# Attention, GRU and experts kernel: the preparation written into the same block as the recurrence, with mean squares from the layer norm's variance and two of four batches prepared inside the first units

## The reference

```
x = x + tanh(g_xattn) * xattn(layernorm(x), ctx)
    # xattn: slots = layernorm(x); k, v = rmsnorm(ctx) @ Wk.T, @ Wv.T; three times:
    #   scores = (rmsnorm(slots) @ Wq.T) @ k.T * D**-0.5
    #   attn = softmax(scores, axis=-2)
    #   attn = attn / (sum(attn, -1) + 1e-6); updates = attn @ v
    #   slots = gru_cell(updates, slots, wih, whh, bih, bhh)
x = x + tanh(g_ffn) * ffn(layernorm(x))
    # ffn: 16 experts, each takes its 512 best tokens; plus a shared expert
```

## Time and profile before

| what | value |
| --- | --- |
| median of 3 runs | 1162.04 us (1161.96 to 1163.13) |
| the profiled execution | 1162.68 us, of which the span is 1160.9 us |
| PE busy | 1101.3 us (95%) |
| DVE, ACT, POOL busy | 69%, 48%, 31% |
| mean granted clock of PE | 0.97 |
| chain that ended last | PE 87%, DVE 6%, ACT 1%, issue 1%, POOL 1% |

### The profile page before, as it was taken

One profiled execution on the slowest core, in us unless ns is written; L12 is line 12 of the kernel. 1 busy time (PEld: TensorE's weight loads), 2 busy tenths in 40 slices (PEclk: granted clock), 3 DMA queues, 4 the chain that ended last, 5 costly groups with the idle time before them and its releaser, 6 DMA issues.

```text
span 1160.9 us, 18197 instructions
## 1 busy us (share of the span) xinstructions
PE 1101.3 (95%) x6151; PEld 951.5 (82%) x6151; DVE 798.2 (69%) x1533; ACT 555.7 (48%) x835; POOL 362.4 (31%) x363
## 2 busy tenths in 40 slices
PE   5659999999999998999999999999999999999996
PEld 3547888888888786888888888888888888888896
DVE  7575777787878986888755666666566666566663
ACT  3252545454545783333354545544455455454542
POOL 6222444444420610000021442342343243243232
PEclk9558999999999999999999999999999999999998
DMA  4310010101032644121274534534544543453421
GB/s 163 100 24 13 1 37 1 36 0 36 0 109 59 197 145 119 22 36 20 38 223 144 145 92 126 144 89 133 145 110 117 137 112 114 138 145 92 127 38 19
DMA packets 60199, 102.96 MB, mean 89 GB/s; under 512 B 11777, under 2 KB 49921, under 8 KB 55809
## 3 DMA queue, kind: packets, MB, share of 16 engines
q1 hardware_dynamic: 41888, 79.11, 21.2%
q0 software_dynamic: 16512, 21.50, 11.5%
q10 hardware_dynamic: 1760, 1.86, 0.5%
HBM read 74.11 MB, written 21.27 MB: 82 GB/s over the span
## 4 chain that ended last, share of the span: by engine, by line
PE 87%; DVE 6%; ACT 1%; issue 1%; POOL 1%; DVEq 0%; ACTq 0%; POOLq 0%
PE wide L1343 28%; PE wide L987 15%; PE down L1357 15%; PE wide L1196 7%; PE down L1208 4%; PE down L1040 3%; PE wide L994 2%; PE wide L996 2%; PE wide L1389 2%; PE side L274 1%; PE side L1329 1%; PE side L1180 1%; PE down L1403 1%; DVE rec_parts L1725 1%; DVE dif L1698 1%
## 5 line engine op out<-in xcount | busy, mean ns | idle before, releaser
L2139 DVE SCALAR_TENSOR_TENSOR hid<-wide,b_up,silu 128x512 f32<-128x512 f32 x120 | 90.1, 751 | 161.7 <-PE wide L1343 154.2
L1343 PE MATMUL wide<-xt_hi,w_hi 128*128 128x512 f32 x480 | 188.4, 393 | 0.0
L1343 PE MATMUL wide<-xt_lo,w_hi 128*128 128x512 f32 x480 | 187.8, 391 | 0.0
L1343 PE MATMUL wide<-xt_hi,w_lo 128*128 128x512 f32 x480 | 187.0, 390 | 0.0
L958 POOL DMA_INDIRECT out_tokens<-y,idx_out x64 | 111.5, 1742 | 222.2 <-DVE y L2120 176.2
L1643 ACT ACTIVATE silu<-wide,b_gate 128x512 f32<-128x512 f32 x120 | 82.3, 686 | 143.6 <-PE wide L1343 142.3
L1357 PE MATMUL down<-w_hi,hid_hi 128*128 128x256 f32 x480 | 136.5, 284 | 0.0
L1357 PE MATMUL down<-w_lo,hid_hi 128*128 128x256 f32 x480 | 135.7, 283 | 0.0
L1357 PE MATMUL down<-w_hi,hid_lo 128*128 128x256 f32 x480 | 135.7, 283 | 0.0
L1652 ACT ACTIVATE hid_hi<-hid 128x512 fp32r<-128x512 f32 x120 | 76.0, 633 | 100.5 <-DVE hid L2139 99.6
L2090 DVE TENSOR_TENSOR w_lo<-raw,w_hi 128x768 fp32r<-128x768 f32 x128 | 121.5, 949 | 2.5 <-ACT w_hi L1617 2.5
(11 more groups left out here) (330 smaller groups left out, 2399.8 us busy)
## 6 DMA issues: line engine op xcount, KB each, us to landing
raw<-in_w_expert SPq DMA_DIRECT2D x32, 1536.0 KB, 7.0
out_tokens<-slots SPq DMA_DIRECT2D x16, 256.0 KB, 3.8
token_rows<-work SPq DMA_DIRECT2D x8, 512.0 KB, 3.0
out_tokens<-y POOLq DMA_DIRECT2D x8, 512.0 KB, 5.9
attn<-rms_c SPq DMA_DIRECT2D x24, 128.0 KB, 2.3
attn<-expo SPq DMA_DIRECT2D x24, 128.0 KB, 2.4
x_first<-in_x SPq DMA_DIRECT2D x8, 256.0 KB, 3.2
work<-in_x SPq DMA_DIRECT2D x8, 256.0 KB, 4.0
```

Source lines behind the costliest of these rows:

```text
L1343: last = nc.tensor.matmul(bank[:, f % 2, :], w[f // HALF_F][:, f % HALF_F, (c + k) * P:(c + k + 1) * P], x_[:, k, :], start=(m == 1), stop ...
L2139: nc.vector.scalar_tensor_tensor(hid[:, f % 2, :], eup[:, f % 2, :], b_up[:, bass.ds(e, 1), f:f + 1].rearrange("p a b -> p (a b)"), silu[: ...
```

## The change

All the preparation moves into the main block; the first block, its `bank` and `turn` PSUM tiles and its closing barrier are gone. All eight groups of x are loaded at the start into `x_raw`, which lies where `slots_lo` will lie; the weights lie where the second half of `slots` and `slots_hi` will be. The root mean squares of the first round come from the layer norm's variance with the same chain of small DVE operations, so no square, no addition and no `sum_squares` is made for the first round. The context is no longer normalised: its reciprocal root `ctx_rstd` goes into the exponential's scale and into the value weights. Groups 4 to 7 are normalised, turned and split inside units 0 to 3 of the recurrence, and the softmax of pair 1 is moved about one unit later in that first half iteration. `vw_hi` and `vw_lo` are now each brought to both partition halves by four DMAs. The hardware loop is written out.

```diff
+        x_raw = Region(O + 65536, O + 98304)("x_raw", [P, KC, T])
...
             @block.sync
             def _(sp):
+                weights(ctx_sb, ctx_tok, l_ctx)
+                load_raw(0)
+                load_raw(1)
+                weights(wq_sb, wq, l_wq)
+                load_raw(2)
+                load_raw(3)
+                weights(wv_sb, wv_t, l_wv)
+                weights(wih_sb, wih_t, l_wih)
+                weights(whh_sb, whh_t, l_whh)
                 for g in range(G1, G):
-                    sp.dma_start(x_tile(g), xv[g]).then_inc(l_x1[g - G1], 16)
+                    load_raw(g)
+                sp.wait_ge(a_own, 1)
+                move_rows(vw_hi, vw_own[:, :, :].bitcast(F32))
+                sp.wait_ge(p_own, 1)
+                move_rows(vw_lo, vw_f)
...
                 def turn_first(g):
-                    pe.wait_ge(n_x1, g - G1 + 1)
-                    if g >= G1 + 2:
-                        pe.wait_ge(s_s0, g - 1)
-                    turn_group(x_tile(g), turn_banks1(g))
+                    pe.wait_ge(*normed(g))
+                    if g >= G1:
+                        pe.wait_ge(s_s0, g)
+                        pe.wait_ge(v_attn, 2)
+                    else:
+                        n = FIRST.index(g)
+                        if n >= 2:
+                            pe.wait_ge(s_lo, n - 1)
...
+                gru_unit(0, 0, 0, 0)
+                gru_unit(0, 0, 0, 1, lambda: turn_first(4))
+                turn_first(5)
+                gru_unit(0, 0, 1, 0, lambda: turn_first(6))
+                turn_first(7)
                 pe.wait_ge(s_s0, G)
-                with pe.Fori(0, ITERS - 1) as it:
-                    half_iteration(it, 0, True, True)
-                    half_iteration(it, 1, True, True)
+                scores(1, 1, (G - 1, G))
+                turn_rms(1)
+                gru_unit(0, 0, 1, 1, lambda: spread_rms(1, 0))
+                spread_rms(1, 1)
+                sum_squares(pe, G, 0, 0, (v_ms, 2))
+                gru_unit(0, 0, 2, 0)
+                gru_unit(0, 0, 2, 1, lambda: column_sums(1))
+                turn_rec(1)
+                sum_squares(pe, G + 1, 0, 1, (v_ms, 2))
+                gru_unit(0, 0, 3, 0, lambda: spread_rec(1))
+                gru_unit(0, 0, 3, 1)
+                sum_squares(pe, G + 2, 0, 2, (v_ms, 2))
+                half_iteration(0, 1, True, True)
+                half_iteration(1, 0, True, True)
+                half_iteration(1, 1, True, True)
...
+                gru_unit(0, 0, 0, 0, None, (lambda: normalise(4),), (lambda: normalise(5),))
+                gru_unit(0, 0, 0, 1, None, (lambda: first_slots(4),), (lambda: first_slots(5),))
+                gru_unit(0, 0, 1, 0, None, (lambda: first_slots(6),), (lambda: first_slots(7),))
...
+                def late_split(g):
+                    sl = slice(g * GROUP, (g + 1) * GROUP)
+                    dve.wait_ge(s_s0, g + 1)
+                    nc.vector.tensor_copy(slots_hi[:, :, sl], slots[:, :, sl]).then_inc(s_hi, 1)
+                    if g not in POOL_LOW:
+                        dve.wait_ge(s_hi, g + 1)
+                        nc.vector.tensor_tensor(slots_lo[:, :, sl], slots[:, :, sl], slots_hi[:, :, sl].bitcast(F32),
+                                                ALU.subtract).then_inc(s_lo, 1)
...
+                gru_group(0, 0, 0, (lambda: normalise(6), lambda: normalise(7)),
+                          (lambda: late_split(4), lambda: late_split(5)))
+                gru_group(0, 0, 1, (lambda: late_split(6), lambda: late_split(7), lambda: spread_steps(1)),
+                          (lambda: scale_scores(1, 0), lambda: scale_scores(1, 1), lambda: maximum(1)))
+                gru_group(0, 0, 2, (lambda: token_sum(1), lambda: csum_reciprocal(1)), (lambda: spread_reciprocal(1),))
+                gru_group(0, 0, 3, (lambda: attention_half(1, 0), lambda: attention_half(1, 1)),
+                          (lambda: attention_lo(1, 0), lambda: attention_lo(1, 1)))
```

More of the change, by code:

```diff
@@ L297, in flamingo_kernel @@
         s_s0 = sem("s_s0")
[L299 to L311, removed]
@@ new lines, in _ @@
+                for h in range(2):
+                    part = pick_f[:, h, :].rearrange("p (b m) -> p b m", b=2)
+                    for sign, base in ((1, -BLK * h), (-1, BLK * h + BLK - 1)):
+                        pool.wait_ge(c_pool, n)
+                        nc.gpsimd.affine_select(out=part, in_=part, compare_op=ALU.is_ge, fill=0.0, base=base,
+                                                pattern=[[-sign * 2 * BLK, 2], [0, MB]],
+                                                channel_multiplier=sign).then_inc(c_pool, 1)
+                        n += 1
@@ L1025, in gru_unit, with scores @@
                     from_attention(gate_x, 4 + c, True).then_inc(m_x, 1)
-                def scores(s, pair, split_before, first=False):
+                def scores(s, pair, split, first=False):
                     if not first:
@@ new lines, in _ @@
+                act.wait_ge(l_vec, 16)
+                for k in range(KC):
+                    last = nc.scalar.activation(pn_t[:, k, :], small_banks[0][:, k * M:(k + 1) * M], ACT.Copy,
+                                                scale=vecs[:, 14 + k:15 + k])
+                last.then_inc(w_pn, 1)
+                act.wait_ge(m_w, 1)
+                nc.scalar.activation(kp_t[:, :, :], small_banks[1], ACT.Copy).then_inc(e_w, 1)
+                act.wait_ge(m_w, 2)
+                act.wait_ge(v_vec, 1)
@@ L1519, in _ @@
+                for n in range(3):
+                    value_weights(n)
+                normalise(1)
+                value_weights(3)
+                first_high(0)
+                first_high(2)
+                normalise(3)
                 copy_rms(0, 0, True)
                 copy_rms(0, 1, True)
+                first_high(1)
+                first_high(3)
+                act.wait_ge(e_w, 7)
+                nc.scalar.activation(vw_own[:, :, :], vw_f[:, :, :], ACT.Copy).then_inc(a_own, 1)
@@ L1828, in _ @@
                 dve.sem_inc(v_new, 1)
[L1829 to L1840 removed]
+                dve.sem_inc(v_ms, 2)
@@ new lines, in aggregate @@
+                def aggregate(stats, mv, var):
+                    st.wait()
+                    for t in range(NT):
+                        st.add(nc.vector.bn_aggr(mv[:, t, :], stats[:, t, :]))
+                    st.wait()
+                    st.add(nc.vector.tensor_scalar(var[:, 0:NT], mv[:, :, 1], LN_EPS, None, ALU.add))
+                    st.do(nc.vector.tensor_scalar(var[:, NT:2 * NT], mv[:, :, 1], 1.0 + RMS_EPS, LN_EPS * RMS_EPS,
+                                                  ALU.mult, ALU.add))
```

666 lines of the change are left out of this document (326 added, 340 removed).

## The result

The changed kernel takes 1146.75 us (median of four runs, 1144.72 to 1148.53), the kernel before 1162.59 us beside it (four runs, 1161.96 to 1163.84). The ratio is 0.9862, with a 95% interval of 0.9838 to 0.9886. It is faster by 15.8 us, which is half of the 31 us that I forecast; 1146.75 lies outside my range. The profiled execution took 1144.72 us, its span is 1143.0 us (1160.9 before).

What follows compares the result with a forecast made beforehand. It took a relay of waits between engines to bound the start and a busy PE everything from 98.26 us on. Terms -41.9 + 3.5 - 0.8 + 8.0 = -31.2 us gave 1131 us, range 1121 to 1143.

Steps and rivals of the forecast that it cites:

- The x that DVE needs ... I take 12.0.: Start of the kernel: the x for the first statistics has landed at 12.0 us, 12.5 at the latest.
- With two more small operations and the root mean square I take 4.5.: Start, on DVE: 4.5 us from the aggregation's start to the first normalisation, against 3.7 before.
- The relay: Chain between engines from reciprocal roots at 17.8 us, through scores at 30.5, to the first attention matmul at 56.4.
- The rival of a shorter relay: Start chain 5 to 8 us shorter and half the waits in the units gone: about 1121 us; chance 17%.
- The new waits, +8.0: First half iteration: PE waits for turns 5 and 7, scores, column sums and attention of pair 1, together +8.0 us.
- the four turns: First half iteration: four turns added on PE at 0.87 us each, +3.5 us.
- the 56 that I had named as a sign of being wrong: Sign against the forecast: `vw` rows landing after 56 us; their moves were to begin near 35 us.
- A clock of 0.5 beyond 60 us: Sign against the forecast: PE's clock at 0.5 later than 60 us in the profile after.
- the rival in which the units run at the low clock: Idle pieces in the units bring the low clock, 10.3 instead of 5.5 us a unit: 1179 us; chance 3%.
- Everything behind it is the same work on a full PE, and I carry the difference unchanged.: From the second half iteration's scores (162.73 us before) to the end, the gain there stays the same.
- Writing out the loop costs or brings nothing.: Hardware loop: writing it out changes nothing; the half iteration with the loop's turn takes 56.73 us, its neighbour 56.60.
- The crowded engines: Units 0 to 3: DVE and ACT cannot carry both works, waits double to 16 us: about 1143 us; chance 22%.

Runs made afterwards that it cites:

- e4: Changed kernel with groups 1 and 3 of x loaded on ScalarE's queue instead of SyncE's; 1145.91 us, ratio 0.9849.
- e2: Changed kernel with ScalarE making pair 1's exponential ahead of group 1's high part and nn in unit 4; 1143.82 us, ratio 0.9819.
- c1: Changed kernel with the edits of e5 and e3 and nine satisfied waits ahead of the expert loop; 1134.19 us, ratio 0.9760.
- e5: Changed kernel with GpSimd's cast and subtraction of the recurrent weights waiting until VectorE has normalised groups 0 and 2; 1140.39 us, ratio 0.9798.
- c2: Changed kernel with all of c1's edits and those of e2, e4 and e6; 1134.43 us, ratio 0.9752.
- c3: Changed kernel with c1's edits and e4's second queue for x; 1135.58 us, ratio 0.9756.
- e1: Changed kernel with GpSimd's cast and subtraction waiting until VectorE has written the first root mean squares; 1146.18 us, ratio 0.9847.
- e6: Changed kernel with e2's edit and TensorE's column sums of pair 1 behind the whole unit instead of between its matmuls; 1143.97 us, ratio 0.9825.
- e7: Changed kernel with satisfied waits ahead of TensorE's expert loop, shifting its code: 1141.32 us with nine, 1146.73 us with 61 (one run each).
- e3: Changed kernel with pair 1's low attention parts made behind unit 6's pre instead of unit 7's; 1145.99 us, ratio 0.9847.

## Why the prediction was wrong, step by step

The prediction has the right sign and mechanism, and misses by 15.75 us in the median, 13.3 in the profiled execution (31.2 forecast, 17.9 gained). By its own steps:

- **"The x that DVE needs ... I take 12.0."** It was 14.07, and DVE's aggregation began at 15.60 instead of 13.3: 2.3 us. I had carried a rate of 386 GB/s over to a row of loads that reached 257 and 200 GB/s in the windows 4:6 and 6:8. What sets the landing is not shown: with two queues (e4) the same windows have 287 and 366, but x is there no earlier than in some executions with one (e2 and c1, aggregation at 14.12). Over nine executions with one queue this step is 0.8 to 2.3 us too short.
- **"With two more small operations and the root mean square I take 4.5."** It took 9.71, and this step failed most. With the cast and subtraction out of the way the chain takes 5.36 (e5; 5.58, 5.58 and 5.23 in c1, c2 and c3), so my reading of the earlier trace rows was 0.9 short; 4.35 are GpSimd's cast and subtraction, shown by e1, where the cost moves with them, and e5, where it goes. I had weighed this very hold-up, for the splits inside the units, from the earlier trace rows, and did not ask what GpSimd does beside the roots. The rule that I quoted (the Trainium skill, SBUF — State Buffer, the section "Who interferes with whom") says that whichever issues first keeps the shared ports for its whole instruction and the other waits it out; the trace agrees, in that the size of DVE's operation, 34 elements, does not matter, but the rest of GpSimd's, up to 3.3 us. The same section of that page of the Trainium skill, SBUF — State Buffer, has VectorE operations in a 2-port mode contend too, which it says `tensor_scalar` can enter; e1's normalisation, eight of these, was held up as well (6.99 us), and whether they ran in that mode no run here shows.
- **The relay** from the roots to the scores was 13.2 instead of 12.7 us, from the scores to the first attention matmul 23.9 instead of 25.9 (the scores began at 38.53): together 1.5 us better. The rival of a shorter relay was right in that much.
- **The new waits, +8.0**, were 8.6; the four turns took 1.06 us each instead of 0.87, +0.8. These steps held. The rows of vw were a near thing: their moves began at 42.64 us and not near 35, and the last landed near 60, behind the 56 that I had named as a sign of being wrong. No wait for them shows, since the first attention matmul was itself late; in c1, where it is at 56.47, they begin at 36.1 and have landed by 53.4.
- **The clock.** I put it at nothing in the sum. "A clock of 0.5 beyond 60 us" stood among the signs of being wrong, and the rival in which the units run at the low clock had 3%. It came for some ten microseconds behind the wait for the token sums. Six slot matmuls take 2.77 us there (`110.77 2.77 PE wide L844 x6`) and 1.37 elsewhere; with the stage 6.0 us longer than forecast and 1.4 of it explained by waits and turns, some 4.5 us are left for it. Two pairs of kernels that have the same program and waits in the stage give the price apart from my forecast: the changed kernel 81.14 us with 10.2 at the low clock, e5 79.61 with 6.8; c3 79.33 with 10.2, c1 76.08 with 3.4. That is 1.5 and 3.3 us for 3.4 and 6.8 us of low clock, and by this rate 4.5 to 5 for 10.2. What makes the clock fall, and for how long, stays open: neither e2 nor e6 kept it up.
- **"Everything behind it is the same work on a full PE, and I carry the difference unchanged."** It was not unchanged, in both directions. Up to the first expert matmul the gain grew from 19.1 to 21.4 us (600.55 - 579.16): the kernel before has a short low stretch in there (0.97 in 440:500, 1.00 now), which accounts for about 1.7 of the 2.3. Then 3.5 us were lost in the expert loop.
- **"Writing out the loop costs or brings nothing."** True for the half iterations (56.60 and 56.64) and false for a loop 400 us later, whose code it moved: e7 gives 3.4 us back.

In sum: 2.3 + 0.9 + 4.35 - 1.5 at the start, 1.4 in waits and turns, 4.5 by the clock, -2.3 and +3.4 behind, 13.1 of the 13.3. The crowded engines, my rival with 1143 us, were not the cause, though the time lies near theirs: DVE and ACT held each other up no more than I had walked through.

That the changed kernel's four runs lie in two pairs, 1144.7 and 1145.0, and 1148.5 twice, would fit two low stretches at 375 and 434 us, present or not. The mean granted clocks of the runs, 0.985 and 0.983 against 0.982 twice, point the same way; only an execution without them was profiled, so this is argued and not shown.

## What to carry to other kernels

Before a small chain of VectorE operations is put on the critical path, look at what GpSimd does in the same microseconds: an operation of 0.2 us took 3.3 here, what was left of GpSimd's, and a wait on GpSimd's side is free where its result is wanted later (one line brought the first attention matmul forward by 4.9 us). Put such work beside VectorE operations that the trace shows undisturbed, here those that read PSUM, and look whether the cost has merely moved, as in e1. Work "behind the change" is unchanged only in its instructions: compare the period of a later loop and the granted clock of later stages before a difference is carried to the end. A difference of two or three microseconds between two profiled executions can be a low stretch in one of them: look at the clock ahead of the edit as well.

## What the runs showed of the hardware

- A turn of TensorE's expert loop costs 0.27 us more or less by where its code lies, with the same instructions: periods of 34.57, 34.30 and 34.30 us with 0, 9 and 61 waits ahead.
- The same wait of 2.6 us was followed by 10.2 us of the low clock in six kernels (c3 among them), by 6.8 in two (e3, e5) and by 3.4 in one (c1); one execution has short low stretches behind waits at 375 and 434 us, another with the same waits has none. When the clock falls was not settled.
- GpSimd's cast (1.5 us) and subtraction (3.5 us) held up VectorE operations on 34 elements, 0.20 us else, until their own ends (1.34 and 3.30 us). In e1 they held up eight normalisations (6.99 instead of 2.67 us). Beside them copies and subtractions that read PSUM took 1.17 and 1.18 us (e5), and in the kernel before an aggregation beside the same subtraction its usual 1.17.
